# Narrow attention: batch 0's query rows by way of DRAM, its mask made at the stage's head, the first whole chunk's split behind the first batch's maxima

## The reference, cut to what matters

```
x = x + tanh(g_xattn[1]) * L1_xattn(layernorm(x), ctx, ctx, ...)
x = x + tanh(g_ffn[1])   * L1_ffn(layernorm(x), rhs)          # products of int8-rounded values
x = x + tanh(g_xattn[2]) * L2_xattn(layernorm(x), ctx, ctx, ..., query_pos, key_pos, mask)
x = x + tanh(g_ffn[2])   * L2_ffn(layernorm(x), ...)
x = x + tanh(g_xattn[3]) * L3_xattn(layernorm(x), ctx, ctx, ...)
x = x + tanh(g_ffn[3])   * L3_ffn(layernorm(x), ...)
```

```
scores = einsum('bhqd,bhkd->bhqk', Q, K) / sqrt(8) - slope[h] * (query_pos - key_pos)
scores = where(mask == 0, -inf, scores);  m = max(scores);  e = exp(scores - m)
out = einsum(e / (1 + sum(e)), V) @ W_o.T
```

## Time and profile before

| | |
|---|---|
| median of 3 executions | 1421.42 us (1418.78 to 1422.36) |
| the profiled execution: its time | 1418.97 us |
| its span in the trace | 1417.2 us |
| busy in the span: PE / DVE / ACT / POOL | 88% / 70% / 58% / 49% |
| granted TensorE clock, mean | 0.924 of full speed |
| layer 1's int8 block (`layer1_int8`) | about 750 to 784 us of the span |
| layer 2's stage | 784 to about 1000 us |
| layer 3's stage | 1166 to about 1392 us |

### The profile page before, as it was taken

The page is one execution under the profiler, slowest core; times in us unless marked ns, Lnnn a source line. Parts: engine busy times, 40 slices in busy tenths (PEclk is TensorE's granted clock), DMA queues, the critical chain, the costliest instruction groups (busy, mean ns, idle before and its releaser), DMA issues. The chain is left out here.

```text
span 1417.2 us, 33719 instructions
## 1 busy us (share of the span) xinstructions
PE 1252.6 (88%) x12564; PEld 751.2 (53%) x12572; DVE 991.2 (70%) x3090; ACT 815.4 (58%) x1206; POOL 698.6 (49%) x651
## 2 busy tenths in 40 slices
PE   5999977936999999999984499999799978999994
PEld 4444444632666666666663155555467753555542
DVE  4988856146667666766657588888366767888866
ACT  2777743424767656665543377777544434777773
POOL 4777622621668667766863455341162008636411
PEclk8999988975999999999996699999999986999996
DMA  4565562634644244234003465450050003434201
GB/s 161 193 230 209 203 241 90 188 110 142 231 164 143 68 162 166 91 111 156 2 1 73 120 181 139 127 114 28 16 119 2 11 9 94 104 77 82 59 8 31
DMA packets 91140, 157.82 MB, mean 111 GB/s; under 512 B 15585, under 2 KB 60796, under 8 KB 87399
## 3 DMA queue, kind: packets, MB, share of 16 engines
q1 hardware_dynamic: 86704, 125.80, 30.0%
q10 hardware_dynamic: 2256, 25.37, 4.7%
q0 software_dynamic: 2032, 4.62, 1.5%
HBM read 99.16 MB, written 50.62 MB: 106 GB/s over the span
## 5 line engine op out<-in xcount | busy, mean ns | idle before, releaser
L2170 ACT ACTIVATE a_probs<-a_psE 128x1024 f32<-128x1024 f32 x256 | 262.3, 1025 | 86.3 <-PE a_psE L2014 82.9
L2216 DVE CUSTOM_DVE_ANT_0 a_junk<-a_psM,a_madd 128x512 bf16<-128x512 f32 x320 | 208.6, 686 | 29.9 <-issue 25.6
L2610 DVE TENSOR_REDUCE a_mx<-a_psM 128x1 f32<-128x512 f32 x236 | 148.2, 669 | 113.6 <-PE a_psM L2434 113.6
L1975 PE MATMUL a_psM<-narrow_k_op,narrow_q_op 57*64 57x512 bf16 (+1 forms) x960 | 192.1, 410 | 18.1 <-DMA narrow_q_op<-narrow_first_parts 11.9
L2571 ACT ACTIVATE a_probs<-a_psE 128x1024 f32<-128x1024 f32 x128 | 130.7, 1025 | 85.6 <-PE a_psE L2456 82.5
L2400 POOL TENSOR_TENSOR a_half_sum<-a_probs 128x1024 f32<-128x1024 f32 x64 | 150.7, 2355 | 32.1 <-ACT a_probs L2571 32.1
L2026 PE MATMUL a_psO<-a_probs,narrow_values 128*32 128x256 f32 x2048 | 163.4, 393 | 1.2 <-ACT a_probs L2170 1.2
L2005 PE MATMUL a_psE<-narrow_q_op,narrow_k_op 60*64 60x256 bf16 (+1 forms) x2048 | 154.9, 280 | 0.0
L2014 PE MATMUL a_psE<-a_maddT,res_identb 64*64 64x512 bf16 x512 | 148.9, 384 | 0.0
L2014 PE MATMUL a_psE<-a_maddT_cross,res_identb 64*64 64x512 bf16 x512 | 146.8, 384 | 0.0
L2452 PE MATMUL a_psE<-a_qT,a_kT 64*128 64x256 f32 x1024 | 133.9, 381 | 0.0
(11 more groups left out here) (421 smaller groups left out, 2657.4 us busy)
## 6 DMA issues: line engine op xcount, KB each, us to landing
wide_k<-a_k_stage SPq DMA_DIRECT2D x32, 512.0 KB, 2.6
a_k_part<-wide_k SPq DMA_DIRECT2D x64, 256.0 KB, 5.0
wide_v<-a_v_stage SPq DMA_DIRECT2D x24, 512.0 KB, 4.1
a_kT<-wide_k ACTq DMA_DIRECT2D x6, 2048.0 KB, 8.3
a_values<-wide_v ACTq DMA_DIRECT2D x6, 2048.0 KB, 9.8
keys<-a_parts SPq DMA_DIRECT2D x96, 64.0 KB, 2.0
narrow_k_op<-keys SPq DMA_DIRECT2D x28, 192.0 KB
narrow_q_op<-a_queries SPq DMA_DIRECT2D x28, 192.0 KB
```

What stands on the lines that cost most here:

```text
L1975: last = pe.matmul(max_bank(s, j, first)[c * n:(c + 1) * n, :], q_op[r][group, s // 2, s % 2 * P + c * n:s % 2 * P + (c + 1) * n], k_op[r] ...
L2170: act.activation(probs[:, head:head + 2, k:k + 2, :], psE[es % 2][:], ACT.Exp).then_inc(exped, 1)
L2216: dve.tensor_tensor_reduce(junk[j][:], max_bank(s, j, first), madd[r][:, t, :], 1.0, -3.0e38, ALU.add, ALU.max, mx[r][:, max_place(h, t):m ...
L2610: dve.tensor_reduce(mx[r][:, at:at + 1], max_bank(2 * p + t, j, first), AX.X, ALU.max).then_inc(max_read, 1)
```

## The change

It has four parts.

1. Batch 0's query rows go through DRAM. `FirstQueries.store` writes `first_parts` in 3 transfers, each part to as many copies as there are combinations of it (3, 2, 1), into `first_scr`. `load_first` waits for them and fetches the rows in 2 transfers. In layer 2 the stores stand at the end of SP's list in `layer1_int8`, the loads at the head of the stage. In layer 3 all five are in the experts' block. ACT issues none any more.
2. In `NarrowConstants.sync`, `load_keys(1)` moves ahead of the store of the positions' parts, and `load_positions(1)` directly behind `load_positions(0)`; the slopes' 6 transfers now stand last.
3. Layer 2's mask of batch 0 is loaded into a buffer of the stage (`mask_first`) and turned into `madd_first` by POOL's first instruction of the stage. DVE waits for it.
4. In both stages POOL's `split_queries(1)` moves from ahead of `split_max(0, 0)` to behind `split_max(0, 1)`. In SP's list `store_queries(v + 1)` moves from ahead of `cross_masks(v + 1)` to behind `maxima(v, 1)`, where it is the last of the batch. What follows it is `load_keys(v + 2)`.

```
 # NarrowBuffers
-    def load_first(self, eng, j, part):
-        for c in range(*RUNS[part]):
-            at = j * GROUP_ROWS + c * HEAD_E
-            eng.dma_start(self.q_op[0][at:at + HEAD_E], self.first_parts[j * GROUP_ROWS:(j + 1) * GROUP_ROWS, part, :]).then_inc(self.first_rows, 16)
+    def load_first(self, sp):
+        sp.wait_ge(self.first_stored, 16 * len(RUNS))
+        for j in range(2):
+            at = j * GROUP_ROWS
+            sp.dma_start(self.q_op[0][at:at + HEAD_ROWS].rearrange("p t q -> p (t q)"),
+                         self.first_scr[:, at:at + GROUP_ROWS].rearrange("c (e t) q -> c e (t q)", e=HEAD_E)).then_inc(self.first_rows, 16)
 # FirstQueries
-    def rows(self, eng):
+    def store(self, sp):
         for part, ready in enumerate((1, 3, 4)):
-            eng.wait_ge(self.cut, ready)
-            for j in range(2):
-                self.nb.load_first(eng, j, part)
+            sp.wait_ge(self.cut, ready)
+            some = slice(*RUNS[part])
+            sp.dma_start(nb.first_scr[some].rearrange("c n q -> n c q"),
+                         nb.first_parts[:, part:part + 1, :].to_broadcast([P, some.stop - some.start, S])).then_inc(nb.first_stored, 16)
 # NarrowConstants.gpsimd, layer 2 only
-        pool.tensor_scalar(self.nb.madd_first[:], self.mask[:], 0.0, -BIG, ALU.is_equal, ALU.mult).then_inc(self.masked, 1)
 # narrow_attention, SP
-                    for part in range(len(RUNS)):
-                        nb.load_first(sp, 0, part)
+                    nb.load_first(sp)
...
-                    if v + 1 < NCHUNK:
-                        sp.wait_ge(split, 4 * (v + 1))
-                        store_queries(sp, v + 1)
                     if v + 1 < B:
                         cross_masks(v + 1)
                     maxima(v, 1)
+                    if v + 1 < NCHUNK:
+                        sp.wait_ge(split, 4 * (v + 1))
+                        store_queries(sp, v + 1)
 # narrow_attention, POOL
+                if cfg.late_rows:
+                    pool.tensor_scalar(nb.madd_first[:], nb.mask_first[:], 0.0, -BIG, ALU.is_equal, ALU.mult).then_inc(first_masked, 1)
...
-                pool.wait_ge(split_first, 4)
-                split_queries(1)
                 for v in range(B):
...
                     split_max(v, 1)
+                    if v == 0:
+                        pool.wait_ge(split_first, 4)
+                        split_queries(1)
 # narrow_attention, ACT
-                if cfg.late_rows:
-                    for part in range(len(RUNS)):
-                        nb.load_first(act, 1, part)
 # narrow_attention, DVE
+                    elif take_max and cfg.late_rows:
+                        dve.wait_ge(first_masked, 1)
```

More of the change, by code:

```diff
@@ L1355, in _ @@
                 def _(sp):
-                    first.rows(sp)
+                    first.store(sp)
+                    res.narrow.load_first(sp)
 HEAD_E = D // HEADS
@@ L1404, in __init__ @@
         self.pos_scr = nc.dram_tensor("pos_parts", [B, 3, S2], BF16).ap()
+        self.first_scrs = [nc.dram_tensor(f"first_queries{i}", [N_COPIES, P, S], BF16).ap() for i in range(2)]
+        self.mask_first = ph.sb("mask_first", [P, QT, S2], I32)
     def load_keys(self, sp, ks, u, r, sem):
@@ L1444, in __init__ @@
         self.made, self.biased, self.cut = (ph.sem(f"first_{n}") for n in ("made", "biased", "cut"))
-        nb.first_rows = ph.sem("first_rows")
+        nb.first_rows, nb.first_stored = ph.sem("first_rows"), ph.sem("first_stored")
+        nb.first_scr = nb.first_scrs[cfg.keys]
     def tensor(self, pe):
@@ L1562, in sync @@
         sp.dma_start(nb.bo[:], io["L3_bo"].unsqueeze(0)).then_inc(self.weights_in, 16)
+        nb.load_keys(sp, self.keys, 1, 1, nb.first_keys)
         sp.wait_ge(self.pos_cut, 5)
@@ L1565, in sync @@
         sp.wait_ge(self.placed, 16)
-        nb.load_positions(sp, 0, 0, nb.first_keys)
+        for u in range(2):
+            nb.load_positions(sp, u, u, nb.first_keys)
         sp.wait_ge(self.slopes_cut, 1)
@@ L1571, in sync @@
                 sp.dma_start(nb.q_op[r][at:at + 9], self.slopes_b[:, j * PAIRS:(j + 1) * PAIRS, :]).then_inc(self.placed, 16)
-        nb.load_keys(sp, self.keys, 1, 1, nb.first_keys)
-        nb.load_positions(sp, 1, 1, nb.first_keys)
         sp.wait_ge(self.placed, 16 * (2 * RING + 1))
@@ L1672, in narrow_attention @@
         if cfg.slopes:
-            mask_i = [ph.sb(f"mask{i}", [P, QT, S2], I32) for i in range(RING)]
+            mask_i = [nb.mask_first] + [ph.sb(f"mask{i}", [P, QT, S2], I32) for i in range(1, RING)]
             maskT_i = [ph.sb(f"maskT{i}", [P, KT, S], I32) for i in range(RING)]
@@ L1815, in _ @@
                             sp.wait_ge(masked, v - 1)
+                        elif v == 1 and cfg.late_rows:
+                            sp.wait_ge(first_masked, 1)
                         if v >= 1:
@@ L1819, in _ @@
                         load_maskT(v + 2)
+                    if v + 1 < B:
+                        cross_masks(v + 1)
+                    maxima(v, 1)
                     if v + 1 < NCHUNK:
@@ L2727, in _ @@
                     norm.gpsimd(pool, c)
-                ahead.finish(pool)
+                pool.wait_ge(ahead.mask_in, 16)
             @block.vector
```

14 lines of the change are left out of this document (5 added, 9 removed).

## The result

The changed kernel takes 1449.56 us (median of 4, 1448.91 to 1450.04), the kernel before 1421.89 (1418.78 to 1423.13). The ratio is 1.0193, with a 95% interval of 1.0174 to 1.0212: 28 us slower. The forecast was 1433, with a range up to 1442. The direction was right, the size less than half of what came.

What follows compares the result with a forecast made beforehand. PE's own work was taken as the bound from batch 1 on, any wait adding to it. 2.7 - 1.9 - 1.5 + 9.0 + 2.3 + 2.4 = 13.0 us gave 1433; own range 1427 to 1439, with rivals 1420 to 1442.

Steps and rivals of the forecast that it cites:

- Head, 2.7: Head of layer 2's stage: a chain of three landings replaces one, PE's first product at 798.1, 2.7 us longer.
- 6 longer: Upper end for layer 2's head: slower landings in both places and 2 us more queueing make it 6 us longer.
- Part 3, nothing: Layer 2's mask at the stage's head: POOL ends it some 3 us before PE's first product, nothing gained.
- Batch 0's cut, -1.9 and -1.5: POOL's cut of batch 0's maxima starts earlier: 1.9 us less in layer 2, 1.5 less in layer 3.
- POOL has 4.09 us of idle time, enough: Layer 2, before split_max(1, 0): POOL's 4.09 us of idle time covers the 3.7 us of the moved split.
- Waits at slot 13, 4.1, 1.6 and 3.3: Layer 2, batches 1 to 3: late stores delay loads and maxima, PE waits 4.1, 1.6 and 3.3 us, together 9.0.
- the group takes 14.7 us from its first issue, whatever stands before it: Layer 2, batch 1's loads: first issue to a_cT's landing stays 14.7 us, so a later start delays the landing equally.
- The clock, 2.4: Layer 2: one of the three new waits, 4.1 us, drops PE's clock to 0.50; 2.4 us added, ends 0 and 9.
- each wait drops the clock: Rival: all three layer 2 waits cost 2.9 us more each, layer 3's a little; 1442 us, chance 0.12.
- Layer 3, 2.3: Layer 3: POOL's cut of batch 1 0.8 us late, PE too, plus 0.5 allowed for each of three batches; 2.3 us.
- Small transfers overtake: Rival: maxima and store packets pass large loads in SP's queue, no slot 13 waits; 1416 us, faster, chance 0.1.
- The loads catch up: Rival: load groups start on an empty queue and take 11 us instead of 14.7; 1422 us, the same, chance 0.2.

Runs made afterwards that it cites:

- e6: Kernel before with part 4 alone, plus the masks of batch v + 2 issued, from batch 1 on, only once maxima(v, 0) have landed: ratio 1.0102.
- e9: Kernel before, real stores in place, plus six extra 512-byte stores behind maxima(v, 1), v = 0 to 2, in both stages: ratio 1.0035.
- e5: Kernel before with only SP's lines of part 4 (chunk stores last in each batch's list), POOL's order as before: ratio 1.0144.
- e2: Changed kernel with part 4 taken back, so parts 1 to 3 alone: ratio 1.0029 to the kernel before.
- e14: The changed kernel run once more, unaltered, to see whether its places of loss repeat: ratio 1.0219 to the kernel before.
- e7: Changed kernel with the maxima's transfers issued by ACT, in its own queue instead of SP's: ratio 1.0359 to the kernel before.

## Why the prediction was right or wrong

The prediction found the place: the stores ahead of the loads delay the loads, the maxima behind them land late, and PE waits at slot 13 of batches 1 to 3 and of no others. Four steps of its sum failed: the length of the group of loads, which it held fixed; the clock, of which it priced one wait out of three; layer 3, for which it took an allowance without a row; and the landings of the head, for which it took the lowest rows.

- **Head, 2.7: 5.05 measured** (about 4.3 between the means over all traces). PE's first product at 798.37 looks like the forecast 798.1, but only because the block had begun 2.1 us early. SP's wait for `pos_parts` took 6.6 us (770.66 to 777.27) and not 4.8: that is 1.6 late counted from the block's start. The last load, counted from the second one's issue at 791.36, took 7.0 us where the lowest row of the keys, 5.3, was used. The steps between came out 0.9 shorter. The choice of minima from the earlier trace rows is the step that failed. The upper end "6 longer" is a slip too: its own terms, 2.7 + 1.3 + 1.3 + 2, give 7.3. And by the rule that the prediction takes from the Trainium skill ("DMA: Bandwidth & Descriptors", section "Why a DMA increments its semaphore by 16 and not by 1") the keys' 24 rows lie on the lowest twelve engines and not on eight. The eight are among them, the sum doesn't use it, and no run shows it.
- **Part 3, nothing:** right; POOL's mask ran from 789.76 to 793.40, ahead of PE's first product.
- **Batch 0's cut, -1.9 and -1.5:** right, -1.66 and -1.52.
- **"POOL has 4.09 us of idle time, enough":** wrong by 1.0. POOL was as late as forecast (it starts the cut 10.5 us behind `maxima(0, 1)`). But the 4.09 us belonged to a batch that began at low clock, 0.58 in its first 3 us. In the changed kernel the clock was at 1.00 there, and DVE's sixteenth read was done 9.4 us behind `maxima(0, 1)` in place of 10.7.
- **Waits at slot 13, 4.1, 1.6 and 3.3, together 9.0:** the place and the transfer were right. Measured are 5.73, 5.22 and 2.50, together 13.45. What failed is "the group takes 14.7 us from its first issue, whatever stands before it". The terms, forecast and measured, in us ("later" is the first key's distance from `maxima(v, 1)`, less the 1.6 of before):

| batch | keys later | group | wait |
|---|---|---|---|
| 1 | 5.9, 4.4 | 14.7, 17.7 | 4.1, 5.73 |
| 2 | 3.7, 4.3 | 14.2, 17.5 | 1.6, 5.22 |
| 3 | 3.7, 3.1 | 15.9, 15.7 | 3.3, 2.50 |

For batches 2 and 3 the forecast group is the landing that the prediction took (862.2 and 888.8) less the first key's issue before (848.0 and 872.9). With the measured terms put into the prediction's own sum the waits come out at 5.6, 5.5 and 2.5. So the form of the sum was right and two of its three group lengths were wrong, by 3 us each; in batch 1 half of that was hidden by a delay taken 1.5 too long. Part of the 3 us is the masks of v + 2 (e6: 1.0 to 1.7). Before, they were issued 2.2 us ahead of the group's landing in batch 1 (at 835.43, behind `maxima(1, 0)`), now 8.3. The rest is argued and not isolated: the stores' 768 KB directly ahead are the candidate, and e9 against e5 fits. Why batch 3's group isn't longer stays open. A group's length also varies without late stores: 16.1, 15.7 and 17.1 in e2, where the keys start on time and PE waits 0.6 us at most.
- **The clock, 2.4:** 9.0 measured, less 1.3 that the kernel before paid and this one doesn't (at the start of its batch 1, where 0.58 over 3 us means 2.5 us at 0.50). At half clock a stretch of PE's work costs half its length, so the 5.0, 6.4 and 6.6 us of low clock behind the three waits cost 2.5, 3.2 and 3.3. That closes the batches: 5.73 + 2.5 + 1.0 (POOL) - 1.3 = 7.9 (7.96 measured), 5.22 + 3.2 = 8.4 (8.47), 2.50 + 3.3 = 5.8 (5.74). Counted by matmuls, 62 in place of 102, it would be 2.4 for 6 us, which is too little. The rival "each wait drops the clock" had this step right. Its time, 1442, was too low as it kept the waits too short.
- **Layer 3, 2.3: 8.0 measured.** "The loads have no positions and no masks beside them; I allow 0.5 for each" was an allowance and not a sum. 5.85 us of it stand in batch 3: waits of 0.79 and 1.78, and then 6.8 us at 0.50. 1.8 stand in batch 1, where PE waits for POOL as long as before (0.24), so the forecast "PE with it" was wrong; there the low clock lasted longer, and 0.54 us of wait came at slot 13. Why it is batch 3 stays open (e14).
- **"Small transfers overtake", 0.1:** false, by e7 as well. **"The loads catch up", 0.2:** two of the three groups got slower instead.

So the sum was 13.0 and is 31.1: head +2.4, waits +4.5, POOL +1.0, clock +5.3, layer 3 +5.7, small pieces +1.3, less the 2.1 ahead of the block.

## What to carry to other kernels

When a transfer is moved, write down for every small transfer near it how many bytes are handed to the DMA engines before it lands, through all queues, those issued shortly behind it included, and price it by that. A landing time read from a trace belongs to the traffic around it then; it is no property of the transfer. Count a mark from the start of its own block, or an unrelated shift will make a wrong term look right. And where PE runs at 99%, price the clock for each stop, not once: the stops of 2.50 to 5.73 us in the changed kernel cost themselves and 2.5 to 3.3 us of low clock again.
